# Attention in two stages on one core: key and value products moved into the step of their own query, and every engine's order set for it

## What is computed

```python
xq = fp8(clip(ln(x) / in_scale))                       # done before the stage
q  = ln_head(linear(xq, wq));   k = ln_head(linear(xk, wk));   v = linear(xv, wv)
p  = softmax(q @ k.T / sqrt(D)); o = p @ v             # per group of 2 query heads
y  = fp8(clip(o / smooth / in_scale))
x  = x + linear(y, wproj) * scale
```

## Time and profile before

| | us |
|---|---|
| three runs, median (lowest to highest) | 1180.33 (1180.01 to 1180.78) |
| the profiled execution | 1176.74 |
| its span | 1175.0 |
| TensorE busy in the span | 903.1 |
| VectorE busy | 946.7 |
| ScalarE busy | 710.1 |
| GpSimd busy | 394.0 |
| first to last matmul of the self stage's query products | 281.9 to 642.4 (start) |
| the same in the cross stage | 681.3 to 1063.9 (start) |

### The profile page before, as it was taken

One profiled execution on the slowest core, in us unless ns is written; L12 is line 12 of the kernel. 1 busy time (PEld: TensorE's weight loads), 2 busy tenths in 40 slices (PEclk: granted clock), 3 DMA queues, 4 the chain that ended last, 5 costly groups with the idle time before them and its releaser, 6 DMA issues. The chain is left out here.

```text
span 1175.0 us, 23858 instructions
## 1 busy us (share of the span) xinstructions
PE 903.1 (77%) x6878; PEld 781.6 (67%) x6878; DVE 946.7 (81%) x2442; ACT 710.1 (60%) x2471; POOL 394.0 (34%) x498
## 2 busy tenths in 40 slices
PE   3610067423999999999999469999999999998638
PEld 3510033212888888888888358888888888887627
DVE  7989989887888888888888558888888888886461
ACT  3454044374877777777778457667667677674303
POOL 0009900000344444444443443333333433333124
PEclk9965588756999999999999779999999999999559
DMA  6022100002000000000000120000000000000400
GB/s 218 1 108 71 36 1 0 0 0 108 2 1 1 0 0 0 0 0 0 0 0 0 41 86 6 6 7 7 4 4 4 9 4 4 0 0 1 148 19 18
DMA packets 18267, 26.96 MB, mean 23 GB/s; under 512 B 1265, under 2 KB 15409, under 8 KB 17457
## 3 DMA queue, kind: packets, MB, share of 16 engines
q1 hardware_dynamic: 17840, 25.41, 6.3%
q0 software_dynamic: 384, 1.05, 0.3%
HBM read 23.83 MB, written 2.62 MB: 23 GB/s over the span
## 5 line engine op out<-in xcount | busy, mean ns | idle before, releaser
L1392 ACT ACTIVATE c_p<-c_kT_sc_ps,c_nmax 128x64 f32<-128x64 f32 x256 | 76.7, 312 | 72.4 <-DVE c_nmax L1257 72.4
L1213 POOL TENSOR_TENSOR c_cat<-c_tb,c_mb 128x512 fp32r<-128x512 bf16 x64 | 74.4, 1162 | 137.5 <-DVE c_tb L1291 137.5
L1213 POOL TENSOR_TENSOR s_cat<-s_tb,s_mb 128x512 fp32r<-128x512 bf16 x64 | 74.3, 1161 | 116.4 <-DVE s_tb L1291 116.4
L1392 ACT ACTIVATE s_p<-s_kT_sc_ps,s_nmax 128x64 f32<-128x64 f32 x256 | 76.8, 312 | 48.5 <-DVE s_nmax L1257 48.5
L1409 PE MATMUL s_qo_ps<-wq,s_xqf 128*128 128x512 f32 x256 | 71.8, 403 | 32.4 <-POOL s_xqf L1195 32.4
L1409 PE MATMUL c_qo_ps<-wq,c_xqf 128*128 128x512 f32 x256 | 72.1, 404 | 16.4 <-DVE wv L645 16.4
L1473 PE MATMUL c_pj_ps<-wp,c_cat 128*128 128x256 f32 x512 | 78.0, 296 | 1.5 <-POOL c_cat L1213 1.5
L1473 PE MATMUL s_pj_ps<-wp,s_cat 128*128 128x256 f32 x512 | 77.4, 295 | 2.2 <-POOL s_cat L1213 2.2
L1339 DVE TENSOR_TENSOR c_yb<-c_qo_ps,c_ism 128x512 bf16<-128x512 f32 x64 | 44.3, 692 | 43.0 <-PE c_qo_ps L1444 43.0
L1218 POOL TENSOR_TENSOR c_pn<-c_p,c_rsum 128x256 f32<-128x256 f32 x64 | 39.3, 614 | 118.1 <-DVE c_rsum L1346 118.1
L1218 POOL TENSOR_TENSOR s_pn<-s_p,s_rsum 128x256 f32<-128x256 f32 x64 | 39.3, 614 | 106.4 <-DVE s_rsum L1346 106.4
(11 more groups left out here) (359 smaller groups left out, 2889.0 us busy)
## 6 DMA issues: line engine op xcount, KB each, us to landing
x_res<-in_x SPq DMA_DIRECT2D x4, 512.0 KB, 5.8
vT<-in_ctxT SPq DMA_DIRECT2D x2, 1024.0 KB, 10.5
tf_work<-in_wqT SPq DMA_DIRECT2D x2, 1024.0 KB, 6.0
tf_work<-in_wprojT SPq DMA_DIRECT2D x2, 1024.0 KB, 5.5
w_work<-in_wqxT SPq DMA_DIRECT2D x2, 1024.0 KB, 6.5
w_work<-in_wkvxT SPq DMA_DIRECT2D x2, 1024.0 KB, 8.0
c_ctx<-in_ctxT SPq DMA_DIRECT2D x16, 128.0 KB, 2.3
w_work<-in_wprojT SPq DMA_DIRECT2D x2, 1024.0 KB, 5.7
```

The lines of the kernel that those rows point to most:

```text
L1213: nc.gpsimd.tensor_tensor(cat[out8.o % 2][:], tb[:], mb[:], ALU.subtract).then_inc(cat_ready, 1)
L1392: nc.scalar.activation(pe_s[:, a * S:(a + 1) * S], sc_ps[:, a * S:(a + 1) * S], ACT.Exp, bias=nmax[:, a:a + 1], accum_out=psum_s[:, a:a + ...
```

## The change

The key and value products of a unit move into the step of its own query product, behind the projection; the key transposes move between them and the query product, and read one of two `kn` tiles. On ScalarE and VectorE the parts of a unit are assigned to steps anew: normalising takes ScalarE's Ln and Exp one unit behind its squares, VectorE's part is one step back, and the maxima, the scaled output and its rounding stand in one step. GpSimd's subtraction stands behind the product with the reciprocals and behind the conversion, and the conversion waits for the query product of the unit before too. The diff, cut:

```diff
-        qn, kn = sb("qn", [P, QW]), sb("kn", [P, KW])
+        qn, kn = sb("qn", [P, QW]), [sb(f"kn{i}", [P, KW]) for i in range(2)]
...
@@ gpsimd
-                    u, soft, out8 = units(i, o, 0, 1, 3)
+                    u, soft, out8 = units(i, o, 0, 3, 4)
...
+                            wait_unit(pool, q_done, u.before(1))
...
@@ vector
-                    u, sm, pv, f8, pj = units(i, o, 0, 1, 2, 3, 4)
+                    u, sm, pv, pj = units(i, o, 1, 3, 4, 5)
...
-                        wait_unit(dve, t_done, u.before(1))
+                        wait_unit(dve, t_done, u.before(2))
...
@@ scalar
-                    q, u, sm, pv = units(i, o, 0, 1, 2, 3)
+                    u, norm, sm, pv = units(i, o, 0, 1, 2, 3)
...
                     if u.live:
                         act.wait_ge(kv_done, u.count(1, 1))
+                        wait_unit(act, var_ready, u.before(1))
                         nc.scalar.activation(sq[:, QW:QW + KW], kv_bank(u)[:, 0:KW], ACT.Square).then_inc(sqk_ready, 1)
...
@@ tensor
-                    u, kv_u, t, pt, pv, pj = units(i, o, 0, 1, 2, 3, 4, 5)
+                    u, t, pt, pv, pj = units(i, o, 0, 2, 3, 4, 5)
```

More of the change, by code:

```diff
@@ L1307, in normalised_key, with scaled_output @@
                                                 ).then_inc(kn_ready, 1)
[L1309 to L1335, removed]
+                    def scaled_output():
                         dve.wait_ge(pv_done, pv.count(1, 1))
@@ L1358, in step @@
                 def step(i, o):
-                    q, u, sm, pv = units(i, o, 0, 1, 2, 3)
[L1360 to L1364, removed]
+                    u, norm, sm, pv = units(i, o, 0, 1, 2, 3)
+                    if norm.live:
+                        chain.at(norm.count(1))
+                        act.wait_ge(var_ready, norm.count(1, 1))
+                        chain(nc.scalar.activation(l6[:], v6[:], ACT.Ln))
+                        wait_unit(act, r_ready, norm.before(1))
+                        nc.scalar.activation(g6[:], l6[:], ACT.Exp, scale=-0.5).then_inc(rs_ready, 1)
+                    if pv.live:
+                        act.wait_ge(max_ready, pv.count(1, 1))
+                        wait_unit(act, pn_ready, pv.before(1))
+                        wait_unit(act, rsum_ready, pv.before(1))
+                        for a in range(4):
+                            nc.scalar.activation(pe_s[:, a * S:(a + 1) * S], sc_ps[:, a * S:(a + 1) * S], ACT.Exp,
+                                                 bias=nmax[:, a:a + 1], accum_out=psum_s[:, a:a + 1]
+                                                 ).then_inc(exp_ready, 1)
                     if sm.live:
@@ L1372, in step @@
                     if u.live:
[L1373 to L1376, removed]
-                        nc.scalar.activation(g6[:], l6[:], ACT.Exp, scale=-0.5).then_inc(rs_ready, 1)
+                        act.wait_ge(q_done, u.count(1, 1))
+                        nc.scalar.activation(sq[:, 0:QW], q_bank(u), ACT.Square).then_inc(sqq_ready, 1)
                     if pv.live:
@@ L1380, in step @@
                         nc.scalar.activation(pT[:], po_ps[:, 0:GU * P], ACT.Copy).then_inc(pT_ready, 1)
[L1381 removed]
+                    if u.live:
+                        wait_unit(act, pv_done, u.before(4))
+                        nc.scalar.activation(v_s[u.o % 4][:], kv_bank(u)[:, KW:2 * KW], ACT.Copy).then_inc(v_ready, 1)
+                    if own_kv and u.live and o in CrossHead.WITH_UNITS:
                         cross_head_act(act, nc, aw, work, chunks, i, o)
[L1383 to L1394 removed]
                 pipeline(act, step, ROUNDS, WIDTH, 3)
@@ L1456, in step @@
                         last.then_inc(tq_done, 1)
-                        pe.wait_ge(kn_ready, t.count(1, 1))
-                        wait_unit(pe, kT_ready, t.before(1))
-                        wait_unit(pe, exp_ready, t.before(1, 4))
-                        for a in range(GU):
-                            last = nc.tensor.transpose(kT_ps[:, a * P:(a + 1) * P], kn[:, a * P:(a + 1) * P], ident[:])
-                        last.then_inc(t_done, 1)
                     if pj.live:
```

115 lines of the change are left out of this document (71 added, 44 removed).

## The result

The changed kernel takes 1149.37 us (median of 4 runs, 1147.06 to 1150.45), the kernel before beside it 1180.17: a ratio of 0.9736, with a 95% interval from 0.972 to 0.9753. Run again beside the experiments it took 1150.41, ratio 0.9755 (0.9741 to 0.9768). The forecast was 1146, with a range of 1138 to 1164, and faster with a chance of 0.89. The profiled execution of after took 1150.45 us (span 1148.5), 26.3 less than that of before (1176.74); the sum in the prediction, made against that one, had 34.7 less. So sign and range are right. The forecast gain of 34.7 us is missed by a ninth by the medians (30.8) and by a quarter by the profiled pair (26.3).

A forecast was written before the change was run, and what follows sets the result against it. Bound: a loop through VectorE and ScalarE, not TensorE. Steps of 5.43 us (self, saving 0.38) and 5.83 (cross, saving 0.24), 56 each, save 34.7 us: 1142.0 by the profiled execution, about 1146 by the median; range 1138 to 1164.

The forecast's parts named there:

- What bounded the kernel, and the loop: Self stage runs at a loop through VectorE and ScalarE; key transposes wait for exponentials, 0.43 us a step.
- (a): TensorE's new order of products and transposes: step floors of 5.33 us in the self stage, 5.80 in the cross stage.
- (b): Self stage: exponentials end at 4.75 us, key transposes come at 5.19; that wait goes, with 0.4 us to spare.
- (c): Probabilities ready at 6.25, wanted at 6.35: margin 0.10 us self, 0.57 cross; two-wait instructions use it up, 0.02 a step.
- (d): GpSimd's token conversion may hold VectorE's rounding addition: 0.08 us a step in the self stage, 0.03 in the cross stage.
- probability transposes wait in every step: Sign named against the forecast: TensorE's probability transposes waiting in every step.
- the addition held for the whole conversion in the cross stage: Sign named against the forecast: VectorE's rounding addition held for the whole of GpSimd's cross-stage conversion.
- Filling and draining: Start and end of each stage: nothing taken, 2 us held either way; growth above 2 us would count against the forecast.
- The longer path: First rival: probabilities' path 0.3 to 0.5 us a step longer, giving 1158 to 1166 us; chance 0.16.
- The slower rival: Second rival: GpSimd holds clip, exponent tile and scaling every step, 0.9 us in all, giving 1207 us; chance 0.07.
- break-even: Added delay on the probabilities' path at which the slower rival's formula gives zero gain: 0.66 us.

The follow-up runs named there:

- 0.66: Changed kernel with two extra VectorE reductions ahead of every unit's reciprocal, 0.66 us more on the probabilities' path: 1179.77 us, ratio 0.9998.
- 0.33: Changed kernel with one extra VectorE reduction ahead of every unit's reciprocal, 0.33 us more on the probabilities' path: 1162.25 us, ratio 0.984.
- 0.98: Changed kernel with three extra VectorE reductions ahead of every unit's reciprocal, 0.98 us more on the probabilities' path: 1211.08 us, ratio 1.0258.

## Why the prediction was right, and where it was not

**What bounded the kernel, and the loop.** Right. With the transposes back the wait returns (1330 us), with the maxima later it returns too (1254), and with neither it is gone. Not tried one by one were the new place of the key and value products, the second key tile and the new place of GpSimd's subtraction.

**(a) TensorE's order.** Floors of 5.367 and 5.833 against 5.33 and 5.80. The 0.05 us taken off because key and value products end in transposes did not come in full: unstalled steps were 5.85 in the cross stage before and, by the prediction's own sum, 5.38 in the self stage. This is 0.035 x 112 = 3.9 us and the whole of what the steady steps missed.

**(b) The margin at the key transposes.** 0.31 measured, 0.4 laid out; right to a tenth.

**(c) The margin at the probabilities.** 0.17 instead of 0.10, and two-wait instructions did not use it up: ordinary steps stall by nothing. The layout itself was close. Its own rows add up to 5.19 + 0.18 + 0.24 + 0.61 = 6.22 for the finished product, where it says 6.25; in an ordinary step of the changed kernel it is 6.23 (query product, reciprocal, GpSimd's product):

```profile
558.72 1.17 PE L1417 MATMUL s_qo_ps<-wq,s_xqf 128*128 128x512 f32 x4
...
563.92 0.18 DVE L1337 RECIPROCAL s_rsum<-s_psums 128x4 f32<-128x4 f32 x1
564.33 0.62 POOL L1214 TENSOR_TENSOR s_pn<-s_p,s_rsum 128x256 f32<-128x256 f32 x1 [1.94 <-DVE s_rsum L1337]
```

The rule for what exceeds the margin was wrong: half goes into a step, not all.

**(d) The conversion.** Right in mechanism and size; neither did the probability transposes wait in every step nor was the addition held for the whole conversion in the cross stage (0.62 us). Charged were 0.10 a step with (c) in the self stage, 0.03 in the cross stage; the means above the floors are 0.109 and 0.029. Inside the self stage, the probability transposes lost 0.29 every fourth step (0.23 laid out) and the projection 0.18 every eighth (0.07 every fourth). In the cross stage the cause was partly another: the held addition also slows the cast.

The Trainium skill states the rule behind this on its page "SBUF — State Buffer", section "Who interferes with whom": the shared pair of ports is locked for a whole instruction by whoever comes first, against VectorE instructions in 2-port modes or with two SBUF inputs. The rows here agree: addition 0.41 to 1.03, scaling 0.17 to 0.68 and 3.12, reduction and instructions with a PSUM input unchanged, and the casts longer where the addition had the pair.

**Filling and draining.** The term that failed: 0 within 2 us assumed, some 4.5 lost in the profiled pair, and the prediction had named more than 2 as a sign against it. "The same operations and the same depth" overlooked that the first unit's chain now has the third unit's products inside it, and, in the cross stage, that they run there at the lower clock; this the traces show, with 2.46 us. How much of the rest is real stays open. By the medians (30.8 and 29.2) at most 1.6 us are missing beyond the steady steps, and the profiled execution of before was 3.4 us faster than the median.

**The rivals.** The longer path did not occur. Its price at 0.5 does not follow from its own terms: 5.33 + 0.40 + 0.10 = 5.83 is no gain in the self stage, but 1.1 us lost where 1.7 are written as gained, so 1169 and not 1166. The slower rival was priced with a rule too steep for ordinary steps and a path too few in the conversion steps. At 0.66 the two errors cancelled, and that its break-even was met (1179.77) is luck. Its formula gives 1157 at 0.33, where 1162 was measured, and 1216 at 0.98, where it was 1211; the 1234 expected before that run was for 1.02 and added the whole excess to a time that has the stalls in it already.

## What to carry to other kernels

When a wait is removed, ask of each remaining loop how many steps it spans: an excess on a loop of two steps costs half as much a step as on a loop of one. Count the work of the next engine too: VectorE was busy 89.74 us of 100 in the self stage, so some 0.6 us a step were free, and with 0.98 more it was the bound. Then look at what VectorE and GpSimd execute at the same moment, and place the long instruction of the one beside instructions of the other that were never held in these traces (reductions and those that read PSUM): that was worth 0.5% for an exchange of two lines. And price the first unit of a stage as a chain of its own, with whatever now stands inside it.

## What the runs showed of the hardware

A VectorE instruction of 0.17 us on 128 x 6 elements took 3.12 us beside a GpSimd instruction of 4.5 us, a hold that no share of busy time shows. The hold goes both ways: where the addition began within 0.02 us of the cast and kept its 0.41 us, the cast took 0.68 us instead of 0.40 (256 columns, the run with 0.66 extra) and 1.11 instead of 0.82 (768 columns, the run with 0.98 extra). A wait of the weight loader of some 0.2 us left the matmuls where they were: 47 such waits, 10.0 us in all and most of them of 0.18, some of 0.3, stand in the self stage of the kernel with the addition first, whose steady steps have no stall.
